# A softmax's sum over twelve heads: four of them delivered by ScalarE's exponentials, eight left to VectorE

## The reference

```
# second stage, heads of 16; third stage, heads of 64 with normalised q and k
scores = jnp.einsum('bqhd,bkhd->bhqk', q, k) * scale
attn = jax.nn.softmax(scores, axis=-1)
out = jnp.einsum('bhqk,bkhd->bqhd', attn, v)
...
# third stage only: each head's output is multiplied by a gate
o = (masked_gates[..., None] * o).reshape(B, N, H * HD)
```

## Time and profile before

| what | value |
|---|---|
| median of three runs | 595.31 us (593.17 to 597.15) |
| the profiled execution | 590.72 us |
| its span, first to last instruction | 588.9 us |
| granted TensorE clock, mean | 0.98 |
| instructions | 10749 |

### The profile page before, as it was taken

The page is one execution under the profiler, slowest core; times in us unless marked ns, Lnnn a source line. Parts: engine busy times, 40 slices in busy tenths (PEclk is TensorE's granted clock), DMA queues, the critical chain, the costliest instruction groups (busy, mean ns, idle before and its releaser), DMA issues.

```text
span 588.9 us, 10749 instructions
## 1 busy us (share of the span) xinstructions
PE 525.0 (89%) x4337; PEld 400.0 (68%) x4337; DVE 418.2 (71%) x910; ACT 311.8 (53%) x520; POOL 98.4 (17%) x85
## 2 busy tenths in 40 slices
PE   4899889778978999999998999999968999899696
PEld 4766567556766676778786666877846677686474
DVE  4145767699568767687868677687828888857982
ACT  0234444555335555767636555866535649544762
POOL 7032400000310224200010124100000022011200
PEclk9799999999999999999999999999997999999999
DMA  9993020000000000100000000000000000000000
GB/s 217 298 209 112 1 61 1 7 2 1 1 0 2 1 2 1 55 8 2 1 21 2 2 1 1 1 1 2 1 21 1 1 2 1 1 1 21 2 1 22
DMA packets 12674, 15.99 MB, mean 27 GB/s; under 512 B 6235, under 2 KB 10048, under 8 KB 12240
## 3 DMA queue, kind: packets, MB, share of 16 engines
q1 hardware_dynamic: 9712, 12.71, 8.7%
q10 hardware_dynamic: 2400, 2.00, 1.1%
q0 software_dynamic: 512, 0.59, 0.5%
HBM read 14.11 MB, written 1.18 MB: 26 GB/s over the span
## 4 chain that ended last, share of the span: by engine, by line
PE 68%; DVE 16%; ACT 8%; POOL 3%; issue 2%; SPq 1%; DMA 1%; ACTq 0%; DVEq 0%; POOLq 0%
PE ps L686 15%; PE ps L999 8%; PE ps L696 8%; PE ps L676 7%; DVE smax L1683 4%; PE ps L1057 4%; PE ps L819 4%; PE ps L1189 3%; PE ps L1169 2%; PE ps L879 2%; PE ps L777 2%; DVE psum L1697 2%; POOL side_wide L1928 2%; PE ps L1145 2%; PE ps L1047 2%
## 5 line engine op out<-in xcount | busy, mean ns | idle before, releaser
L1683 DVE TENSOR_REDUCE smax<-ps 96x12 f32<-96x1152 f32 x32 | 43.2, 1349 | 25.8 <-PE ps L1047 19.9
L1354 ACT ACTIVATE pr<-ps,less 96x96 f32<-96x96 f32 x112 | 28.6, 334 | 25.9 <-DVE less L1685 25.9
L1364 ACT ACTIVATE pT<-ps 96x1152 f32<-96x1152 f32 x28 | 31.5, 1126 | 15.0 <-PE ps L1057 15.0
L1697 DVE TENSOR_REDUCE psum<-pr 96x12 f32<-96x1152 f32 x28 | 37.5, 1339 | 2.0 <-ACT pr L1359 1.9
L1057 PE MATMUL ps<-w_ident,pr 96*96 96x96 f32 x336 | 33.3, 249 | 3.0 <-DVE pr L1709 2.1
L1057 PEld LDWEIGHTS ps<-w_ident,pr 96*96 96x96 f32 x336 | 28.2, 127 | 8.1 <-DVE pr L1709 4.0
L1391 ACT ACTIVATE squares<-ps 128x1536 f32<-128x1536 f32 x12 | 17.4, 1451 | 29.3 <-PE ps L696 23.4
L1928 POOL TENSOR_TENSOR side_wide<-attn,w_mask 128x1024 f32<-128x1024 f32 (+1 forms) x12 | 22.2, 1868 | 58.1 <-ACT attn L1248 52.2
L1047 PE MATMUL ps<-b_kB,heads 32*96 32x192 f32 x192 | 20.2, 376 | 11.9 <-ACT b_kB L1334 6.7
L1796 DVE TENSOR_REDUCE ss<-squares 128x24 f32<-128x1536 f32 x12 | 21.0, 1749 | 11.2 <-ACT squares L1391 11.2
L676 PE MATMUL ps<-w_cqkv,side_c 64*96 64x384 f32 (+1 forms) x96 | 27.4, 500 | 0.0
(11 more groups left out here) (357 smaller groups left out, 1322.9 us busy)
## 6 DMA issues: line engine op xcount, KB each, us to landing
x_in<-in_xT SPq DMA_DIRECT2D x3, 768.0 KB, 4.4
b_kB<-in_cqkv SPq DMA_DIRECT2D x1, 1152.0 KB
w_cqkv<-in_cqkv SPq DMA_DIRECT2D x1, 864.0 KB
out<-side_c ACTq DMA_DIRECT2D x3, 288.0 KB, 2.5
w_cqkv<-in_cqkv SPq DMA_DIRECT2D x1, 855.0 KB
heads<-in_xT ACTq DMA_DIRECT2D x3, 256.0 KB, 4.5
side_in<-in_patchT SPq DMA_DIRECT2D x3, 192.0 KB, 4.0
side_tok<-in_tok_ff SPq DMA_DIRECT2D x2, 288.0 KB, 6.6
```

The source lines that it names most:

```text
L1354: m = act.activation(w.y.pr[:, s % 2, h * N:(h + 1) * N], t[0:N, h // 4, h % 4 * N:(h % 4 + 1) * N], ACT.Exp, scale=head ** -0.5, bias=les ...
L1364: act.activation(w.y.pT[:, :, :].rearrange("p (b h) t -> p b (h t)", b=3), t[0:N, :, 0:4 * N], ACT.Copy)\
L1683: dve.tensor_reduce(mx, t, AX.X, ALU.max).then_inc(w.S[stage + "_sub"], 1)
L1697: dve.tensor_reduce(psum[:, s % 2, :], e, AX.X, ALU.add).then_inc(w.S[done], 1)
```

## The change

Each of the four single-head activations gets a second output: the sum of its results along the row, which is the softmax's denominator of that head, goes to its column of `psum`. VectorE's sum then covers the first eight heads only. The reciprocal, the product, the semaphores, the buffers and the order of the units stay as they are.

```
                 for h in range(DVE_LESS, NH):
                     m = act.activation(w.y.pr[:, s % 2, h * N:(h + 1) * N], t[0:N, h // 4, h % 4 * N:(h % 4 + 1) * N], ACT.Exp,
-                                       scale=head ** -0.5, bias=less[:, s % 2, h - DVE_LESS:h - DVE_LESS + 1])
+                                       scale=head ** -0.5, bias=less[:, s % 2, h - DVE_LESS:h - DVE_LESS + 1],
+                                       accum_out=psum[:, s % 2, h:h + 1])
                 m.then_inc(w.S[stage + "_exp"], 1)
...
                 dve.wait_ge(w.S[stage + "_exp"], w.upto(stage + "_exp", w.count(stage), 2 * s + 2))
-                dve.tensor_reduce(psum[:, s % 2, :], e, AX.X, ALU.add).then_inc(w.S[done], 1)
+                dve.tensor_reduce(psum[:, s % 2, 0:DVE_LESS], e[:, 0:DVE_LESS], AX.X, ALU.add).then_inc(w.S[done], 1)
                 dve.wait_ge(w.S[done], w.upto(done, w.count(stage), steps * s + 1))
                 dve.reciprocal(rec[:, s % 2, :], psum[:, s % 2, :]).then_inc(w.S[done], 1)
```

## The result

The changed kernel takes 601.49 us (median of four runs, 600.18 to 601.88) against 594.24 us of the kernel before in the same session: a ratio of 1.0116, interval 1.0065 to 1.0167. With 12 more runs on another chip it was 600.56 us against 595.59 us, ratio 1.0087, interval 1.0057 to 1.0117. So it is slower by about 1%: 7 us in the first session, 5 in the second. The forecast was 599.3 us in a range of 592 to 607.

A forecast was written before the change was run, and what follows sets the result against it. The chain that ended last, 68% TensorE, was taken to bound the kernel. Shorter sums -3.5, exponentials +5.6, wait at 121 us +0.85, pair at 558 us +0.02, queued evacuations +1: +4.0 us, so 599.3 us, range 592 to 607.

The forecast's parts named there:

- What bounds the kernel: No engine is full; the chain of work that ended last bounds it: TensorE 68%, VectorE 16%, ScalarE 8%.
- the seven places where the chain runs through the exponentials: Seven of 32 softmax steps have ScalarE's four single-head exponentials on the chain; longer ones cost there: 7 x 0.80 = 5.6 us.
- What it takes away: VectorE's sums cover 96x768 instead of 96x1152, each 0.39 us shorter: 12.4 us of its work, 3.5 us on the chain.
- 9 x 0.39 = 3.5 us: Gain on the chain from its nine VectorE sums, each 0.39 us shorter.
- the nine sums: Nine of the 32 VectorE softmax sums were pieces of the chain, so only these were to save time, 3.5 us.
- the time can't fall below it: The old chain stays a chain after the change; its new durations, -3.5 and +5.6 us, set a floor.
- What it adds: Each of 128 ScalarE activations delivers a sum, by an instruction of about 0.20 us; added cost 0 to 1.22 us a step.
- one side, 0.80 us a step: The read between ScalarE's exponentials overlaps only with the next: 0.20 us each; the forecast's case, chance 0.42.
- the case to which I gave 0.22: Rival: the read overlaps both neighbouring exponentials, 0.38 us a step, no change at 595.3 us; chance 0.22.
- -3.5 + 2.7 + 0.4 + 0.4: Both-sided overlap's sum: shorter sums, seven places' exponentials, wait at 121 us, queued evacuations; 0 us in all.
- x: Time each single-head exponential gains from start to start; from about 0.27 us the slowdown was to pass 1%.
- Not hidden at 121 us: Second attention, first group, second sample: the sum newly waits 0.85 us for ScalarE and is on the chain.

The follow-up runs named there:

- gain alone: Kernel before, but VectorE sums eight heads, activations deliver no sums and the four other denominators are a constant: 593.66 us against 595.53, ratio 0.9953.
- cost alone: Changed kernel, but activations deliver their sums to an unused tile and VectorE sums all twelve heads: 599.87 us against the kernel before's 595.53, ratio 1.0078.

## Why the prediction came out as it did

- **What bounds the kernel.** Right in the main. Five of the seven places where the chain runs through the exponentials lie in the stretch with the full clock, and 1.66 of the 1.99 us of lag there arose at them; the change without six of the seven places lost its cost. The other two places aren't separated from the clock or from their neighbours.
- **What it takes away.** The size of a sum was right: 939 ns, 0.40 us less, where 0.39 was forecast. The term 9 x 0.39 = 3.5 us was wrong: gain alone is worth 1.0 us. The step that failed is taking a chain's pieces times their saving as time saved. It is only an upper bound of the gain, down to the next path, and I hadn't looked how far behind that one was. In the changed kernel no sum is on the chain at all: at 568 us it ran through L1145 and the copies out, as with gain alone, and where the first of the nine sums had stood, through TensorE's products and the copy at L1311:

```profile
118.26 3.77 PE ps L676 x16
122.03 0.98 PE ps L696 x12
123.00 2.15 PE ps L686 x8
125.15 0.02 issue
125.18 1.26 ACT attn L1311 x3
```

The sentence "the time can't fall below it" was right, and I used the bound as if it were the value. In its place: 1.0 us (0.6) for gain alone, because the next path, through ScalarE and TensorE, was 0.4 us behind at the last pair.
- **What it adds.** That an instruction of its own delivers the sum, of the length of an activation with hardly any columns: right, 197 ns against 0.20 us. Its overlap: wrong choice. I took one side, 0.80 us a step; it is both sides, 0.37 us a step, the case to which I gave 0.22. Four exponentials and their reads fill 1.38 us, not 1.8, and ScalarE's busy time rose by 10.8 us, not 25. The Trainium skill's figures in "ScalarE: Activation LUTs" (section "What ACT_TABLE_LOAD costs") led to an estimate of 0.38 us, and the trace agrees with 0.37. The Trainium skill's rule of two instructions in "VectorE: DVE Perf Modes" (section "Two Vector instructions with no wait between them") is written of VectorE; the trace shows the same on ScalarE, 128 reads of 197 ns. That the read must wait for the end of its exponential was an argument from how it ought to work; the rows had neighbours overlapping everywhere, and that was the better evidence.
- **The sum.** For 0.38 us a step the prediction's own working gave 0 us: -3.5 + 2.7 + 0.4 + 0.4. Measured at the same clock: +3.1. For cost alone the same working has 2.7 + 0.4, and no wait at 121 us, since the sum before it is as long as it was (121.94 + 0.38 against 122.28): 3.1 us, and measured were +3.3 (0.6): right. So the difference lies in the gain, 1.0 us where 3.5 were put, and in the changed kernel not even that: cost and gain alone add up to 2.3 us, 0.8 less than its 3.1. That 0.8 is within the uncertainty of the three together (about 1 us), but the steps at 507 us show where such a loss arises. The forecast of +4.0 us was near the time by luck: too dear a read made up for a gain that wasn't there, and a lower clock came on top. A slip of no weight: by the working's own terms the sum passes 1% at an x of about 0.24 us, not 0.27.
- **Not hidden at 121 us.** The wait came, the loss is not shown. The sum there waits for ScalarE, 0.72 us in the profile, and the four waits of this sort in the changed kernel are 3.9 us together (1.9 in two before). But this sum was no longer on the chain, which the prediction took for granted: from the second maximum to the third (117.05 and 125.28 us before) the changed kernel loses 0.35 us and gain alone, without any reads, 0.26. The row:

```profile
124.98 0.95 DVE L1698 TENSOR_REDUCE psum<-pr 96x8 f32<-96x768 f32 x1 [0.72 <-ACT pr L1360]
```

- **The clock.** Missing. Of the 5.5 us between the medians of all runs, 2.4 are a lower clock. In one and the same kernel its mean varies from 0.963 to 0.983 from run to run, which is 9 us by the slope. How much of the lower mean belongs to the change stays open. I took it for granted from one profile, which happened to be at the upper end of what the kernel before shows.

## What to carry to other kernels

A piece of the chain that gets longer costs up to its full length (0.37 us at four of five places here, 0.18 at one); one that gets shorter gives at most the distance to the next path, so look for that path before you count the gain. Here it was 0.4 us behind at the pair looked at, and it ran through the very instructions to which the work was moved. A sum that an activation delivers costs a further instruction, 0.09 us after overlap beside others on ScalarE: it can be worth it only where VectorE's reduction is waited for and ScalarE isn't. Confined to the nine steps of 32 whose sum was on the chain it gave 0.8 us (0.6) at the same clock, and nothing that the medians show. Where time and granted clock go together as they do here, compare kernels at the same clock before a difference of under 1% is put down to the work.

## What the runs showed that was not expected

- A 197 ns instruction adds only 0.09 us between two exponentials, although it delivers the sum of the one ahead.
- The mean granted clock goes with most of the scatter of one kernel: 80 undisturbed runs of the kernel before, from 590.5 us at 0.98 to 599.6 us at 0.963, along 4.6 us for 0.01.
- TensorE's clock may fall to 1.2 GHz or stay at 2.4 GHz after the same idle time ahead of the same instructions (61 us). Fourteen dummy products in idle stretches lifted its mean in the kernel before from 0.971 to 0.978, and with them it was 0.4% faster (0.9962, interval 0.9935 to 0.9989).
